# Fewer feed-forward items per step in the first half of a softmax-statistics loop, more in the second

## The chip, the cores and the metric

The kernel runs on all 8 cores of one Trainium2 chip, each core on its own two sequences of the batch of 16. The metric is device time in microseconds of the slowest core.

## The reference

One layer adds to its input x (16 x 2048 x 1024, float32) an attention block and a feed-forward block, both on the same layer norm of x:

```python
xn = _layernorm(x, axis=-1)
x = x + attn(xn, W_kqv, W_o) + ffn(xn, W_r, W_k, W_v, mu_r, mu_k)
# attn: 16 heads of 64, rotary embedding on Q and K, causal softmax(QK^T/8) V, then @ W_o.T
# ffn:  xr = mu_r*xn + (1-mu_r)*xn_prev ; xk = mu_k*xn + (1-mu_k)*xn_prev
#       r  = sigmoid(xr @ W_r.T) ; k = square(relu(xk @ W_k.T)) ; out = r * (k @ W_v.T)
```

## The kernel before

Each core works through 8 tiles of 512 tokens, four to a sequence: `for seq in range(2): for J in range(4)`. J says how much causal history the tile has: its keys fill J+1 chunks of 512. A tile is worked in this order:

1. the output projection of the tile before (`wo_emit`, L759), then the K, Q and V projections (L377 and L434);
2. the **statistics loop** (L552 to L622), 16 heads x 4 query blocks of 128 = 64 steps, s = 4h + qtl. A step computes the scores of one query block against all its keys: on TensorE one matmul of 64 rows for each chunk of 512 keys (L567; for J = 3 L591 and L610), the last chunk cut to 128 (qtl+1) columns; on VectorE the causal mask is added to its diagonal block (L573, L597); on ScalarE an exponential over the row, whose accumulated sum is all that is kept (L578; L602 and L616). Score banks are reused after one to three steps, depending on J;
3. the softmax sums become an extra row of Q, and the attention loop proper runs (L699 scores, L709 exponential, L686 product with V).

The feed-forward work of the tile is a list of 246 small closures, `ffn_work`, each of which issues about one instruction. After every step of the statistics loop `drain_ffn(k)` takes the next k of them off the list, so that they stand behind that step's matmuls on TensorE's queue, behind its mask add on VectorE's and behind its exponential on ScalarE's. The engines work their queues strictly in the order written; the only waits are on semaphores. The list in order:

- one subtraction over the whole tile (L455) and 8 multiply-adds of 512 columns (L459), on VectorE: they make the input `xrk` of the r projection from `call`;
- the r projection: 64 matmuls of 128 rows and 512 columns (L476), after each 8 of them an epilogue: Tanh on ScalarE (L486) and a scaling on VectorE (L489);
- 8 multiply-adds on VectorE (L512). They overwrite `xrk` with the input of the k projection, so they wait for the last matmul of the r projection, and the first matmul of the k projection waits for the last of them;
- the k projection: 64 matmuls and 8 epilogues of two VectorE instructions (L495, L499) which write `call`; the v projection needs all of them;
- the v projection: 64 matmuls and 8 epilogues of one VectorE instruction (L505); a last addition (L519).

The matmuls of the projections alternate between PSUM banks 6 and 7, by groups of 8. Twelve weight loads (one for 16 matmuls, SyncE's queue, in the first tile GpSimd's with a store behind it) stand in the list 30 items ahead of their first use, into five buffers. Whatever is left of the list after step 63 is issued by `drain_ffn(n_ffn)`.

With the numbers of before, 3 items per step for s < 32 and 7 after that, the list falls on the steps so:

| steps | items |
|---|---|
| 0 to 3 | two loads, L455, the 8 of L459, 1 matmul |
| 4 to 28 | the other 63 matmuls of the r projection, its epilogues, 4 loads |
| 29 to 31 | the 8 of L512, 1 matmul of the k projection |
| 32 to 53 | the other 127 matmuls, their epilogues, 6 loads, L519 |
| 54 to 63 | none |

Of the kernel before, what the change touches and what calls it, by code (L numbers as in the profile page):

```python
# [133 lines left out]
def build_program():  # L134
# [223 lines left out]
    for seq in range(BSEQ):  # L358
        for J in range(NJ):
# [186 lines left out]
            def drain_ffn(k):  # L546
                while ffn_i[0] < n_ffn and k > 0:
                    ffn_work[ffn_i[0]]()
                    ffn_i[0] += 1
                    k -= 1  # L550

            for h in range(H):  # L552
                for qtl in range(4):
                    s = 4 * h + qtl
# [29 lines left out]
                    else:  # L584
# [24 lines left out]
                        for chn in (0, 1):  # L609
# [9 lines left out]
                            accum_out=sgm[:, 4 * h + qtl: 4 * h + qtl + 1]),  # L619
                          reads=bksL + ["consts"],  # L620
                          writes=["attn0", "attn1", "sgm"])
                    drain_ffn(3 if s < 32 else 7)  # L622
            drain_ffn(n_ffn)
            if ln_phases:
                ln_phases[0]()
# [231 lines left out]
if __name__ == "__main__":  # L857
    nc = build_program()
    print("built ok, instructions:", sum(1 for _ in nc.all_instructions()))
```

How the kernel before makes its waits and increments, by code:

```python
            def run(eng):  # L118
                for s in by_eng[ename]:
                    for sm, v in s.waits:
                        eng.wait_ge(handles[sm], v)
                    inst = s.fn(eng)
                    if s.inc_on:
                        inst.then_inc(handles[s.sem], s.inc)
```

## Time and profile before

| | |
|---|---|
| time, median of 2 runs | 3136.86 us (3132.43 to 3141.3) |
| the profiled execution | 3133.19 us |
| its span on the slowest core (core 2) | 3131.6 us |
| spans of the 8 cores | 3100.7 to 3131.6 us |
| PE busy | 2264.8 us (72%) |
| ACT busy | 1351.3 us (43%) |
| DVE busy | 1246.2 us (40%) |
| granted clock, mean over the span | 0.752 (core 2) |

PE is TensorE, ACT is ScalarE, DVE is VectorE, POOL is GpSimd and SP is SyncE. A granted clock of 1.00 is 2.4 GHz and 0.50 is 1.2 GHz; a value between them is a mean over a stretch that has both. The clock in force decides how long a matmul takes, so a busy share of PE means little without it. A step of the statistics loop starts where the first weight load of its score matmul (L567 or L591) starts; all stretches below are cut at such starts.

### The profile page before, as it was taken

To read this page: it belongs to the slowest core of one execution; us is meant where nothing else is said; L and a number is where in the kernel's file an instruction comes from. 1 tells how busy PE (TensorE), PEld (TensorE's weight loads), DVE (VectorE), ACT (ScalarE), POOL (GpSimd) and SP (SyncE) were. 2 spreads that over 40 slices of the span, in tenths; PEclk is the share of its full clock that TensorE was granted. 3 is DMA by queue.
4 is the path that set the end of the run, shared out by engine and by line. 5 is a ranking of instruction groups with operands and counts; after the bars stand their busy time and mean duration, and the time that the engine had idled before them with its cause. 6 is when DMAs were issued, how large, how long until landed. Compare 5 with 4: busy or idle time off the path is not lost.

```text
span 3131.6 us, 33119 instructions; the slowest of 8 cores (3100.7 to 3131.6 us)
## 1 busy us (share of the span) xinstructions
PE 2264.8 (72%) x8148; PEld 780.8 (25%) x8232; DVE 1246.2 (40%) x2429; ACT 1351.3 (43%) x2729; POOL 101.9 (3%) x125
## 2 busy tenths in 40 slices
PE   1466577677886886977886656767868778798787
PEld 0122131222322222222232212222322222312232
DVE  5444554444432344222344455444443233613122
ACT  0033305551365632776631330444316655077674
POOL 0210010000000001000000000000010000100000
PEclk8787586867677787578788857876776778858687
DMA  4696052103311024100024203310141100500000
GB/s 74 88 168 122 1 151 62 50 0 101 88 34 41 1 75 101 34 24 31 1 81 108 67 9 105 93 56 10 67 108 44 46 1 14 148 26 23 28 1 27
DMA packets 83743, 180.67 MB, mean 58 GB/s; under 512 B 5592, under 2 KB 50792, under 8 KB 81512
## 3 DMA queue, kind: packets, MB, share of 16 engines
q1 hardware_dynamic: 34448, 121.78, 11.5%
q0 software_dynamic: 49120, 56.77, 11.3%
q8 instruction: 84, 1.38, 0.2%
q14 instruction: 91, 0.75, 0.1%
HBM read 153.23 MB, written 31.59 MB: 59 GB/s over the span
## 4 chain that ended last, share of the span: by engine, by line
PE 54%; DVE 19%; issue 9%; DMA 8%; ACT 8%; POOL 1%; DVEq 0%; ACTq 0%; POOLq 0%; SPq 0%
PE ps L476 13%; PE ps L686 11%; PE ps L699 9%; PE ps L567 6%; PE ps L759 4%; DMA qtil<-call 3%; PE ps L610 3%; DVE call L395 3%; ACT attn L578 3%; PE ps L591 2%; DMA ktil<-call 2%; DVE srowt L736 2%; ACT p L709 2%; PE ps L377 2%; DVE attn L731 1%
## 5 line engine op out<-in xcount | busy, mean ns | idle before, releaser
L709 ACT ACTIVATE p<-ps 128x512 bf16<-128x512 f32 (+3 forms) x1280 | 589.7, 533 | 471.1 <-PE ps L699 469.4
L578 ACT ACTIVATE attn<-ps 128x128 bf16<-128x128 f32 (+11 forms) x384 | 331.9, 864 | 880.8 <-DVE ps L573 589.0
L686 PE MATMUL ps<-p,vtok 128*65 128x512 bf16 (+3 forms) x1280 | 487.6, 419 | 102.4 <-DVE p L716 46.8
L699 PE MATMUL ps<-qtil,ktil 65*128 65x512 bf16 (+3 forms) x1280 | 425.8, 431 | 48.6 <-DMA qtil<-augh 48.6
L476 PE MATMUL ps<-xrk,wbuf 128*128 128x512 bf16 x984 | 338.5, 466 | 50.2 <-DVE xrk L512 40.9
L377 PE MATMUL ps<-xn,wbuf 128*128 128x512 bf16 x1008 | 254.5, 398 | 147.3 <-DVE qtil L403 100.9
L567 PE MATMUL ps<-ktil,qtil 64*128 64x512 bf16 (+3 forms) x768 | 254.3, 426 | 128.1 <-ACT attn L578 59.1
L716 DVE TENSOR_TENSOR p<-p,tri 128x128 bf16<-128x128 bf16 x512 | 109.3, 225 | 577.2 <-ACT p L709 570.6
L686 PEld LDWEIGHTS ps<-p,vtok 128*65 128x65 bf16 x1280 | 162.9, 128 | 410.5 <-issue 380.1
L602 ACT ACTIVATE attn<-ps 128x640 bf16<-128x640 f32 (+3 forms) x128 | 110.6, 864 | 233.4 <-PE ps L610 201.1
L573 DVE TENSOR_TENSOR ps<-ps,maskadd 128x128 f32<-128x128 f32 x384 | 107.6, 295 | 254.0 <-PE ps L567 252.9
L699 PEld LDWEIGHTS ps<-qtil,ktil 65*128 65x128 bf16 x1280 | 138.5, 113 | 227.3 <-issue 178.0
L377 PEld LDWEIGHTS ps<-xn,wbuf 128*128 128x128 bf16 x1024 | 97.4, 102 | 304.4 <-issue 215.8
L476 PEld LDWEIGHTS ps<-xrk,wbuf 128*128 128x128 bf16 x1024 | 85.1, 106 | 303.4 <-issue 261.4
L395 DVE TENSOR_TENSOR call<-ps,rsigt 128x512 bf16<-128x512 f32 x128 | 88.5, 691 | 140.7 <-DMA ktil<-call 89.8
L434 PE MATMUL ps<-wbuf,xn 128*128 128x256 bf16 x1024 | 118.4, 275 | 32.1 <-DMA wbuf<-wkqvt 22.4
L616 ACT ACTIVATE attn<-ps 128x1024 bf16<-128x1024 f32 x128 | 131.1, 1024 | 19.1 <-PE ps L591 0.4
L476 PE MATMUL ps<-call,wbuf 128*128 128x512 bf16 x500 | 128.9, 389 | 13.9 <-DVE call L499 12.4
L759 PE MATMUL ps<-attn,wbuf 128*128 128x512 bf16 x496 | 131.5, 424 | 4.8 <-DVE attn L670 3.2
L567 PEld LDWEIGHTS ps<-ktil,qtil 64*128 64x128 bf16 x768 | 59.3, 102 | 301.1 <-issue 292.9
L610 PE MATMUL ps<-ktil,qtil 64*128 64x512 bf16 x256 | 113.9, 539 | 24.2 <-ACT attn L602 14.7
L670 DVE TENSOR_TENSOR attn<-attn,ps 128x512 bf16<-128x512 bf16 x64 | 44.0, 687 | 211.0 <-PE ps L666 209.1
(96 smaller groups left out, 1819.1 us busy)
## 6 DMA issues: line engine op xcount, KB each, us to landing
wbuf<-wtmp SPq DMA_DIRECT2D x196, 512.0 KB, 3.8
y<-outb POOLq DMA_DIRECT2D x8, 2048.0 KB, 7.5
wtmp<-wbuf SPq DMA_DIRECT2D x28, 512.0 KB, 6.8
ktil<-call POOLq DMA_DIRECT2D x32, 256.0 KB, 9.0
qtil<-call POOLq DMA_DIRECT2D x32, 256.0 KB, 9.6
outb<-x POOLq DMA_DIRECT2D x7, 1024.0 KB, 19.8
wbuf<-wkqvt POOLq DMA_DIRECT2D x12, 512.0 KB, 19.8
rsigt<-ropemaps SPq DMA_DIRECT2D x8, 512.0 KB, 4.1
```

Source lines behind the costliest of these rows:

```text
L377: A("T", lambda e, slot=slot, fc2=fc2, ci=ci, bk=bk: e.matmul(bank(bk), wb3[slot][:, ci, 128 * fc2:128 * fc2 + 128], xn3[:, ci, 1:513], st ...
L395: A("V", lambda e, gch=gch, bk=bk: e.tensor_tensor(out=call3[:, gch, :], in0=bank(bk), in1=mapblk[:, 512:1024], op=OP.mult), reads=[bkey, ...
L434: A("T", lambda e, slot=slot, tt=tt, ci=ci, bk=bk: e.matmul(ps[:, 512 * bk: 512 * bk + 256], xn3[:, ci, 1 + 128 * tt:1 + 128 * tt + 128], ...
L476: "T", lambda e, holder=holder, fc2=fc2, ci=ci, bk=bk, rhs3=rhs3: e.matmul(bank(bk), wb3[holder["slot"]][:, ci, 128 * fc2:128 * fc2 + 128] ...
L567: A("T", lambda e, h=h, qtl=qtl, chn=chn, N=N, base=base: e.matmul(ps[:, 512 * (base + chn): 512 * (base + chn) + N], qt_ap[0:64, 512 * h ...
L578: A("S", lambda e, kext=kext, h=h, qtl=qtl, base=base: e.activation(attn[:][:, 0:kext], ps[:, 512 * base: 512 * base + kext], AF.Exp, scal ...
L610: A("T", lambda e, h=h, qtl=qtl, chn=chn, pL=pL: e.matmul(ps[:, 512 * (pL + chn): 512 * (pL + chn) + 512], qt_ap[0:64, 512 * h + 128 * qtl ...
L616: A("S", lambda e, h=h, qtl=qtl, pL=pL: e.activation(attn[:][:, 0:1024], ps[:, 512 * pL: 512 * pL + 1024], AF.Exp, scale=1.0 / 32.0, accum ...
L686: A("T", lambda e, h=h, kti=kti, qs=qs, pb=pb, j=j, nkt=nkt: e.matmul(ps[0:65, 512 * (2 + j) + qs: 512 * (2 + j) + 512], vt_ap[:, 65 * H * ...
L699: A("T", lambda e, h=h, kti=kti, qs=qs, sbk=sbk: e.matmul(ps[:, 512 * sbk + qs: 512 * sbk + 512], kt_ap[0:65, T * h + 128 * kti: T * h + 1 ...
L709: A("S", lambda e, kti=kti, qs=qs, sbk=sbk, pb=pb: e.activation(p2[pb][:, qs:512], ps[:, 512 * sbk + qs: 512 * sbk + 512], AF.Exp, scale=0 ...
L759: A("T", lambda e, slot=slot, fc2=fc2, dc=dc, bk=bk: e.matmul(bank(bk), wb3[slot][:, dc, 128 * fc2:128 * fc2 + 128], attn3[:, dc, :], star ...
```

## The change

The two numbers of the drain after each step are altered, and nothing else: 2 items for s < 32 instead of 3, 8 items from s = 32 on instead of 7.

```diff
@@ -619,7 +619,7 @@
                             accum_out=sgm[:, 4 * h + qtl: 4 * h + qtl + 1]),
                           reads=bksL + ["consts"],
                           writes=["attn0", "attn1", "sgm"])
-                    drain_ffn(3 if s < 32 else 7)
+                    drain_ffn(2 if s < 32 else 8)
             drain_ffn(n_ffn)
```

By the count of the list, the items now fall on the steps so:

| steps | items |
|---|---|
| 0 to 5 | two loads, L455, the 8 of L459, 1 matmul |
| 6 to 31 | 44 matmuls of the r projection, 5 epilogues, 3 loads |
| 32 to 34 | 19 matmuls of the r projection, its last 3 epilogues, 1 load, 1 of L512 |
| 35 | 7 of L512, 1 matmul of the k projection |
| 36 to 54 | the other 127 matmuls, their epilogues, 6 loads, L519 |
| 55 to 63 | none |

## Rows read from the trace of the kernel before

**Rows 1.** The profile's page: clock in 40 slices; the chain by engine; weight loads.

```profile
PEclk8787586867677787578788857876776778858687
PE 54%; DVE 19%; issue 9%; DMA 8%; ACT 8%; POOL 1%; DVEq 0%; ACTq 0%; POOLq 0%; SPq 0%
wbuf<-wtmp SPq DMA_DIRECT2D x196, 512.0 KB, 3.8
```

**Rows 2.** Busy time by stretch: steps 0 to 5; J=0 and J=3.

```profile
core 2: us, PE busy (x) PEld busy (x) DVE busy (x) ACT busy (x) POOL busy (x), PEclk, DMA share, GB/s
176.61:190.12 13.51, 3.77 (x17) 1.25 (x15) 10.06 (x17) 2.48 (x10) 1.75 (x2) 0.61 1.17 214
...
1223.65:1239.96 16.31, 12.07 (x29) 2.75 (x30) 9.44 (x15) 10.94 (x22) 0.00 (x0) 0.51 0.27 77
```

**Rows 3.** Busy time by stretch: steps 6 to 28; J=0 to 3, all eight.

```profile
190.12:215.40 25.28, 22.00 (x81) 6.15 (x81) 8.26 (x27) 15.74 (x50) 2.62 (x3) 0.94 0.93 173
483.53:522.73 39.20, 35.06 (x104) 7.21 (x104) 10.41 (x31) 26.62 (x53) 0.00 (x0) 0.72 0.12 41
831.54:886.38 54.84, 51.65 (x127) 10.85 (x127) 10.98 (x31) 36.56 (x54) 0.00 (x0) 0.56 0.09 29
1239.96:1307.99 68.03, 65.05 (x149) 13.65 (x150) 11.08 (x30) 52.13 (x101) 0.00 (x0) 0.50 0.07 24
...
sum 371.03, PE 339.86 PEld 75.08 DVE 81.10 ACT 261.27 POOL 2.62; mean PE 42.48 PEld 9.39 DVE 10.14 ACT 32.66 POOL 0.33
```

**Rows 4.** Busy time by stretch: steps 29 to 31; J=0 and all eight.

```profile
215.40:226.81 11.41, 1.49 (x7) 0.40 (x6) 8.31 (x16) 3.96 (x14) 0.87 (x1) 0.72 0.88 184
...
sum 83.06, PE 29.16 PEld 5.65 DVE 58.79 ACT 45.61 POOL 0.87; mean PE 3.64 PEld 0.71 DVE 7.35 ACT 5.70 POOL 0.11
```

**Rows 5.** Busy time by stretch: steps 32 to 53; J=0, J=3, all eight.

```profile
226.81:264.95 38.14, 36.23 (x146) 12.84 (x149) 19.20 (x44) 10.94 (x42) 3.18 (x4) 0.95 0.65 111
...
1318.02:1373.18 55.16, 51.90 (x211) 16.73 (x215) 19.46 (x45) 43.77 (x85) 0.00 (x0) 0.95 0.09 30
...
sum 375.28, PE 357.15 PEld 117.89 DVE 155.05 ACT 206.84 POOL 3.18; mean PE 44.64 PEld 14.74 DVE 19.38 ACT 25.85 POOL 0.40
```

**Rows 6.** Busy time by stretch: steps 54 to 63 and the sums' end, all eight.

```profile
sum 161.66, PE 84.99 PEld 15.95 DVE 56.30 ACT 116.97 POOL 0.00; mean PE 10.62 PEld 1.99 DVE 7.04 ACT 14.62 POOL 0.00
```

**Rows 7.** Timeline (start, duration), PE, J=3: six matmuls before and after the clock rises.

```profile
1320.03 2.74 PE L476 MATMUL ps<-xrk,wbuf 128*128 128x512 bf16 x6
...
1323.71 1.47 PE L476 MATMUL ps<-xrk,wbuf 128*128 128x512 bf16 x6
```

**Rows 8.** Timeline, all engines, J=0: between the r and the k projection.

```profile
218.41 0.59 ACT L486 ACTIVATE ps<-ps 128x512 f32<-128x512 f32 x1
219.11 0.69 DVE L489 TENSOR_SCALAR rsigt<-ps 128x512 bf16<-128x512 f32 x1 [2.22 <-ACT ps L486]
219.71 0.29 DVE L573 TENSOR_TENSOR ps<-ps,maskadd 128x128 f32<-128x128 f32 x1
219.91 2.45 DVE L512 SCALAR_TENSOR_TENSOR xrk<-call,mu2s,xn 128x512 bf16<-128x512 bf16 x3
...
226.79 0.59 PE L476 MATMUL ps<-xrk,wbuf 128*128 128x512 bf16 x1 [8.17 <-DVE xrk L512]
```

**Rows 9.** Timeline, ACT, steps without items: exponentials four steps apart, J=0, 2, 3.

```profile
270.65 0.28 ACT L578 ACTIVATE attn<-ps 128x128 bf16<-128x128 f32 x1
273.36 0.28 ACT L578 ACTIVATE attn<-ps 128x128 bf16<-128x128 f32 x1
...
952.91 1.13 ACT L578 ACTIVATE attn<-ps 128x1152 bf16<-128x1152 f32 x1 [0.23 <-DVE ps L573]
960.12 1.13 ACT L578 ACTIVATE attn<-ps 128x1152 bf16<-128x1152 f32 x1 [0.20 <-ACT attn L578]
...
1382.30 0.70 ACT L602 ACTIVATE attn<-ps 128x640 bf16<-128x640 f32 x1 [0.20 <-PE ps L610]
...
1391.98 0.70 ACT L602 ACTIVATE attn<-ps 128x640 bf16<-128x640 f32 x1 [0.20 <-PE ps L610]
```

## The prediction

> **What bounds the kernel now.** I began with the page. TensorE ends most of the chain (54%), and its granted clock in the 40 slices swings between 0.5 and 0.9 [rows 1]. The list is in every case the same 246 items, so a time can only change through three things: the clock at which the moved matmuls run, what ScalarE and VectorE can do beside them, and the waits at the seams. So I cut the statistics loop of all eight tiles at the step starts and read busy time and clock of each stretch.
>
> Steps 6 to 28 (2 to 3 items of matmul each): PE is busy 65.05 of 68.03 us at J = 3, all of it at the lower level of the clock, 1.2 GHz; at J = 2 the mean grant is 0.56, at J = 1 0.72 and at J = 0 0.94 [rows 3]. Steps 29 to 31 belong to VectorE: 8.31 us busy of 11.41 at J = 0, with PE busy 1.49 [rows 4]. Steps 32 to 53 (7 items) run at 0.95, nearly all at 2.4 GHz, with PE busy 36.23 of 38.14 us at J = 0 and 51.90 of 55.16 at J = 3 [rows 5]. After the list has run dry the step is ScalarE's: at J = 3 four steps take 1391.98 - 1382.30 = 9.68 us, 2.42 each; at J = 2 1.80; at J = 0 0.68 [rows 9]. For J = 1 I interpolate 1.2.
>
> The price of one feed-forward matmul at either level: six take 2.74 us at the low one and 1.47 at the high one [rows 7]. A single one at the low level takes 0.59 [rows 8], so the spacing there is (2.74 - 0.59)/5 = 0.43 us and 0.16 of each burst is its end running out; at the high level the spacing is (1.47 - 0.16)/6 = 0.22 us.
>
> **The change part by part.** Counts of items are those of the two tables ahead.
>
> *Steps 0 to 5 hold 5 matmuls fewer.* VectorE's work before the first matmul is unchanged but for two more mask adds of 0.29 us [rows 8]; the other steps' scores pass beside it. At J = 0 before, 2.95 us lay between the first matmul (with the DVE chain about 10.6 us long, from 10.06 us busy) and step 6 at 13.51 [rows 2]; six matmuls at 0.43 were in it, now one: -2.5 and +0.6, so -2.0. At J = 1 and 2 the scores of two more steps also pass under VectorE: -3.2 and -3.8. At J = 3 ScalarE's 2.42 a step takes over, five of them and a start of about 1: 13.0 for 16.31, so -3.3. Two sequences: 2 x 12.3 = **-24.6**.
>
> *Steps 6 to 31: three steps more, 14 matmuls fewer (44 for 58), 3 epilogues fewer.* At J = 3 what is not a feed-forward matmul costs (68.03 - 58 x 0.43)/23 = 1.88 a step. After: 68.0 + 3 x 1.88 - 14 x 0.43 = 67.6; some 0.6 less for the missing epilogues, 67.0. ScalarE would need 26 x 2.42 and five times Tanh's 0.59 = 65.9, so it binds almost equally, and the removed matmuls buy nothing more. J = 2: 54.84 + 3 x 1.31 - 6.0 = 52.8; a bit over half of its steps could lose the clock's better moments, so 53.7. J = 1: 39.20 now (37.3 in the other sequence). All at 1.2 GHz the same reckoning, 44 x 0.43 plus 26 x 0.91, gives 42.6; all at 2.4 ScalarE's floor of 26 x 1.2 and some epilogues gives 33. J = 0: 31.5 and 23.5 in the same way, against 25.28 now. In each J fewer columns pass per step, and the rows say that the stretch with a smaller part of feed-forward matmuls among its PE work is granted less (0.94, 0.72, 0.56, 0.50 for J = 0 to 3, at the same three items) [rows 3]. So I let each J fall towards the next one: J = 1 40, J = 0 27. Sum 2 x (27 + 40 + 53.7 + 67) = 375.4 against 371.0: **+4.4**.
>
> A rule that speaks against this part is in the Trainium skill, page "TensorE: Matmul & The Clock Gate", section "A second HAM failure mode: psum-queue depth-cycling": small idle times of PE between groups of matmuls make the clock swing between its levels, and the cost is paid in the bursts after. The grant of 0.72 at J = 1 agrees with it. By the rule alone J = 0 and J = 1 would be at the low level throughout, and this part would be +18 instead of +4.
>
> *Steps 29 to 31 become step 35.* From the Tanh of the last epilogue to the first k matmul 226.79 - 218.41 = 8.4 us pass at J = 0: Tanh, scaling, eight multiply-adds and three mask adds [rows 8]. The chain is what it was but for two mask adds: 7.8, with the matmuls at both ends 8.4. What changed is that three steps' scores and exponentials passed beneath it, and now one does; that is in the step counts. At J = 2 and 3 the Tanh stands behind its step's own exponentials, so I take 8.9 and 9.5 there. 2 x 35.2 = 70.4 for 83.1: **-12.7**. All else queued on VectorE waits: mask 35, so ScalarE idles some 5 us and PE 7.
>
> *The dense stretch.* Steps 32 to 34 and 36 to 54 are 22 steps as before, with 19 matmuls more. At 2.4 GHz they cost 19 x 0.216 = 4.1 a tile, +32.8. That stretch now starts with r matmuls, straight from the low clock (J = 1 to 3), and after step 35's idle PE climbs a second time. Before, the clock rose 4.7 us after the idle at J = 3 (between the two rows of [rows 7]; work began at about 1318.0). 4 to 4.5 us at half speed lose 2.2: six tiles, and 1 at J = 0: +15.2. At J = 3 ScalarE has slack no more under PE's longer steps, which gives 1.5 back twice: -3. Sum **+45.0** on 375.3 [rows 5].
>
> *The last steps:* one fewer in each tile at ScalarE's floor, 0.68 + 1.2 + 1.80 + 2.42, twice: **-12.1** (of 161.7 [rows 6]).
>
> *At nothing:* the weight loads. They keep their lead of 30 items. Eight items take at least 1.9 us, so the lead is 7 us against a landing of 3.8 [rows 1]. Without that cover a load would cost PE the difference at 12 places a tile. In the first tile GpSimd loads from float32 instead; PE's whole idle time in the dense stretch there is 38.14 - 36.23 = 1.9 us [rows 5], so no load is late by more than that now, and its lead stays. Nothing moves past a DMA issue that another part waits for.
>
> **Sum:** -24.6 + 4.4 - 12.7 + 45.0 - 12.1 = 0.0 on a span of 3131.6 and an execution of 3133.2. The median of the runs stands 3.7 above that execution, so 3137.
>
> **Rivals.**
> *A, the slower side: the clock.* Steps 6 to 31 stay at 1.2 GHz at J = 0 and 1 (2 x (4.5 + 2.6 + 1) = +16), and both climbs of the dense stretch take twice as long (+13). For it: J = 3 and mostly J = 2 do so today; against: at J = 0 0.94 is far from it. With something for ScalarE waiting behind step 35, 3160. It decides as soon as J = 0 is granted under 0.6 in steps 6 to 31.
> *B, faster: the matmuls saved are saved.* J = 0 and 1 keep their grants (2 x (3.5 + 6) = -19), and the first climb takes no loss at some tiles: 3115. For it: 0.94 at J = 0 leaves the low level only a moment there. Against: a smaller share of matmuls.
> *C, much slower: the dense stretch stays low after step 35.* 113 matmuls x 0.21 in eight tiles = +190, 3325. Against it: after an equal idle of 8.17 us [rows 8] the stretch is granted 0.95.
> *D, the change does nothing at the seams:* the 8 multiply-adds hidden as before would leave out the loss of step 35; excluded by their order, since only one step is left beside them.
>
> **How the numbers follow.** My forecast, gains and losses within 12 us of each other, 0.5; A 0.24; B 0.22; C 0.02; D and the rest 0.02. The predicted time is 3137. The unknown terms are the grants (-19 to +16), the second climb (-13 to +13) and step 35 (8 x 1 either way); they don't all fall on one side, and the runs of before differ by 9. Range 3112 to 3163, which takes in A and B. A measurement of this kernel can tell about 2%, 63 us, from no change; that is 8 us a tile, and only C reaches it on the slow side, nothing on the fast side. Faster 0.01, same 0.96, slower 0.03.
>
> **What would show it.** Right: steps 6 to 31 at J = 3 take 66 to 68 us; step 35 8.4 to 9.5; the idle of L476 put down to L512 grows from 8.17 at J = 0 only little there but to 6 or 7 at J = 3; steps 32 to 54 without 35 take 5 to 8 us more at every J, with two climbs of the clock at J = 1 to 3; J = 2 and 3 win a little in all, J = 1 loses. Wrong: a grant over 0.85 at J = 1 in steps 6 to 31 (B), under 0.6 at J = 0 (A), or step 35 under 7 us, which would mean that its chain is not serial.

## The result, and the profile after

| | before | after |
|---|---|---|
| time, median of all runs | 3136.49 us (11 runs) | 3164.70 us (12 runs) |
| ratio, 95% interval | | 1.009 (1.0068 to 1.0113) |
| the same kernel timed again beside another set of before | 3134.15 us (34 runs) | 3173.27 us (11 runs), 1.0107 (1.0073 to 1.0142) |

By the ratios the change makes the kernel 28 to 34 us slower. That is within the 2% of which the prediction gave "same" 0.96, but it is a clear loss where 3137 was forecast, and 1.7 us outside the range. Some executions are disturbed and longer, among them the first profile of the changed one (3210.59 us, with the granted clock at 0.81 for 575 to 765 us of each core, a value that the trace of before never shows), and the ratios leave them out. All rows of after below are from the second profile, `after_again`; where rows are of core 2, so are those of before. The marks of all stretches, before and after, stand 0.50 us ahead of the first weight load of their step; the lengths are those of the steps.

The page of `after_again`, slowest core (core 1): span, PE's busy time, clock, chain by engine, and the matmuls of the projections (L476) with what PE waited for. The last line is the same group before, core 2.

```profile
span 3171.7 us, 33173 instructions; the slowest of 8 cores (3138.6 to 3171.7 us)
PE 2336.8 (74%) x8232; PEld 789.5 (25%) x8232; DVE 1250.9 (39%) x2429; ACT 1350.5 (43%) x2729; POOL 101.9 (3%) x125
PEclk8777585867667687588787757686775877858687
PE 57%; DVE 18%; issue 8%; ACT 8%; DMA 7%; POOL 1%; DVEq 0%; ACTq 0%; POOLq 0%; SPq 0%
L476 PE MATMUL ps<-xrk,wbuf 128*128 128x512 bf16 x1024 | 381.8, 494 | 92.7 <-DVE xrk L512 65.2
...
L476 PE MATMUL ps<-xrk,wbuf 128*128 128x512 bf16 x984 | 338.5, 466 | 50.2 <-DVE xrk L512 40.9
```

ACT's and DVE's busy times are those of before. PE has the same instructions (the trace of before has 984 of the 1024 matmuls of L476) and takes longer for them, 494 ns for 466 by the mean of this group. The stretches show where. First steps 6 to 31 of the changed kernel on core 2 (the columns are those of [rows 2]): J = 0 to 3, the second J = 0, and all eight.

```profile
181.23:213.04 31.81, 30.83 (x69) 5.88 (x71) 10.07 (x30) 17.07 (x56) 1.75 (x2) 0.50 0.75 160
480.61:523.72 43.11, 41.97 (x95) 6.57 (x97) 10.19 (x30) 27.93 (x58) 0.00 (x0) 0.50 0.07 25
830.02:887.15 57.13, 53.03 (x120) 10.42 (x123) 10.38 (x30) 39.02 (x58) 0.00 (x0) 0.50 0.06 19
1238.10:1310.45 72.35, 64.83 (x147) 12.34 (x149) 10.67 (x31) 57.81 (x111) 0.00 (x0) 0.50 0.05 15
1707.90:1734.52 26.62, 25.50 (x68) 5.51 (x70) 8.46 (x27) 15.73 (x52) 0.00 (x0) 0.63 0.13 40
...
sum 404.43, PE 376.21 PEld 69.75 DVE 81.00 ACT 282.55 POOL 1.75; mean PE 47.03 PEld 8.72 DVE 10.13 ACT 35.32 POOL 0.22
```

Against [rows 3]: J = 1 has lost its high clock altogether (0.72 to 0.50), J = 0 most of it (0.94 to 0.50 and 0.63). By the mean of the eight cores the grants were 0.94, 0.80, 0.58 and 0.50 and are 0.60 and three times 0.50. At J = 0 six of the sixteen tiles stay at 0.50 throughout and take 31.8 us, the others rise for a part of the stretch. J = 3 had no high clock to lose, and still takes 72.35 us.

The sums over the eight tiles of the other stretches, in order: steps 0 to 5, 32 to 34, 35, 36 to 54, 55 to the end of the loop.

```profile
sum 93.62, PE 41.62 PEld 10.02 DVE 75.87 ACT 51.68 POOL 1.75; mean PE 5.20 PEld 1.25 DVE 9.48 ACT 6.46 POOL 0.22
sum 68.77, PE 66.16 PEld 20.24 DVE 18.86 ACT 39.10 POOL 0.87; mean PE 8.27 PEld 2.53 DVE 2.36 ACT 4.89 POOL 0.11
sum 76.74, PE 9.99 PEld 2.22 DVE 55.08 ACT 24.76 POOL 0.87; mean PE 1.25 PEld 0.28 DVE 6.89 ACT 3.09 POOL 0.11
sum 359.89, PE 343.38 PEld 117.06 DVE 150.67 ACT 176.69 POOL 3.18; mean PE 42.92 PEld 14.63 DVE 18.83 ACT 22.09 POOL 0.40
sum 149.13, PE 74.72 PEld 14.04 DVE 51.56 ACT 106.02 POOL 0.00; mean PE 9.34 PEld 1.76 DVE 6.44 ACT 13.25 POOL 0.00
```

Set against the terms of the prediction, in us. Beside core 2 stand means of the cores' own sums, of all eight and of cores 4 to 7 alone: in this execution cores 0 to 3 were granted 0.81 for 104 to 151 us each, cores 4 to 7 never.

| term | forecast | core 2 | mean of 8 cores | mean of cores 4 to 7 |
|---|---|---|---|---|
| steps 0 to 5 | -24.6 | -26.1 | -25.5 | -25.8 |
| steps 6 to 31 for 6 to 28 | +4.4 | +33.4 | +32.7 | +32.0 |
| step 35 for 29 to 31 | -12.7 | -6.3 | -5.6 | -4.6 |
| the dense stretch | +45.0 | +53.4 | +47.8 | +43.2 |
| the last steps | -12.1 | -12.5 | -12.6 | -12.6 |
| sum | 0.0 | +41.8 | +36.8 | +32.2 |

Two terms failed, the second by 28 us and the third by 7 to 8. A mean over the cores by J shows that the failure is spread evenly: the whole statistics loop takes 105.3, 128.2, 155.7 and 184.8 us at J = 0 to 3, where it took 100.5, 123.6, 150.9 and 180.6. That is 4.2 to 4.8 us in every tile (3.4 to 4.5 on cores 4 to 7), whatever its clock was before, which suggests more than one cause.

Below, a tile's stretch without rows is such a mean of the eight cores from their traces.

### The profile page after: what moved, and what is told of

The parts are those of the page before. It is cut to its first block, busy times and chain, and to the rows that moved or that the text cites. A ratio compares the mean times of both kernels' runs of the same rounds, so it can differ in the third digit from the quotient of the medians.

```text
span 3209.1 us, 33173 instructions; the slowest of 8 cores (3180.6 to 3209.1 us)
## 1 busy us (share of the span) xinstructions
PE 2396.2 (75%) x8232; PEld 806.4 (25%) x8232; DVE 1251.5 (39%) x2429; ACT 1354.2 (42%) x2729; POOL 101.8 (3%) x125
## 4 chain that ended last, share of the span: by engine, by line
PE 60%; DVE 17%; issue 8%; ACT 7%; DMA 6%; POOL 1%; DVEq 0%; ACTq 0%; POOLq 0%; SPq 0%
PE ps L476 15%; PE ps L686 11%; PE ps L699 9%; PE ps L567 7%; PE ps L759 4%; PE ps L377 3%; PE ps L610 3%; DMA ktil<-call 2%; PE ps L591 2%; PE ps L434 2%; DVE call L395 2%; DVE srowt L736 2%; ACT p L709 2%; DMA qtil<-call 2%; ACT attn L578 2%
## 5 line engine op out<-in xcount | busy, mean ns | idle before, releaser
L476 PE MATMUL ps<-xrk,wbuf 128*128 128x512 bf16 x1024 | 391.0, 505 | 91.0 <-DVE xrk L512 64.8
L377 PE MATMUL ps<-xn,wbuf 128*128 128x512 bf16 x1024 | 279.1, 429 | 133.9 <-DVE qtil L403 96.7
L567 PE MATMUL ps<-ktil,qtil 64*128 64x512 bf16 (+3 forms) x768 | 279.4, 462 | 60.8 <-ACT attn L578 44.2
L602 ACT ACTIVATE attn<-ps 128x640 bf16<-128x640 f32 (+3 forms) x128 | 110.7, 865 | 252.3 <-DVE ps L597 125.4
L476 PEld LDWEIGHTS ps<-xrk,wbuf 128*128 128x128 bf16 x1024 | 89.8, 109 | 339.7 <-issue 315.5
L434 PE MATMUL ps<-wbuf,xn 128*128 128x256 bf16 x1024 | 131.3, 295 | 28.3 <-DMA wbuf<-wkqvt 19.4
L476 PE MATMUL ps<-call,wbuf 128*128 128x512 bf16 x512 | 139.3, 415 | 12.4 <-DVE call L499 12.4
L759 PE MATMUL ps<-attn,wbuf 128*128 128x512 bf16 x512 | 139.2, 436 | 3.2 <-DVE attn L670 3.2
```

Of the source, the lines that this page charges most:

```text
L377: A("T", lambda e, slot=slot, fc2=fc2, ci=ci, bk=bk: e.matmul(bank(bk), wb3[slot][:, ci, 128 * fc2:128 * fc2 + 128], xn3[:, ci, 1:513], st ...
L434: A("T", lambda e, slot=slot, tt=tt, ci=ci, bk=bk: e.matmul(ps[:, 512 * bk: 512 * bk + 256], xn3[:, ci, 1 + 128 * tt:1 + 128 * tt + 128], ...
L476: "T", lambda e, holder=holder, fc2=fc2, ci=ci, bk=bk, rhs3=rhs3: e.matmul(bank(bk), wb3[holder["slot"]][:, ci, 128 * fc2:128 * fc2 + 128] ...
L567: A("T", lambda e, h=h, qtl=qtl, chn=chn, N=N, base=base: e.matmul(ps[:, 512 * (base + chn): 512 * (base + chn) + N], qt_ap[0:64, 512 * h ...
L759: A("T", lambda e, slot=slot, fc2=fc2, dc=dc, bk=bk: e.matmul(bank(bk), wb3[slot][:, dc, 128 * fc2:128 * fc2 + 128], attn3[:, dc, :], star ...
```

## The experiments

**Which of the two numbers, and which tiles.** Each kernel is the one of before with this one line changed.

```diff
-                    drain_ffn(3 if s < 32 else 7)
+                    drain_ffn(2 if s < 32 else 7)                    # first_only
+                    drain_ffn(3 if s < 32 else 8)                    # second_only
+                    drain_ffn((2 if s < 32 else 8) if J < 2 else (3 if s < 32 else 7))   # low_J
+                    drain_ffn((2 if s < 32 else 8) if J >= 2 else (3 if s < 32 else 7))  # high_J
```

`after_again`: 

> The changed kernel once more, for a profile beside those of the next runs. Timed it was 1.009 of before. Its first profile holds the tiles J = 0 and 1 at a granted 0.50 to 0.6 in steps 6 to 31 (before: 0.94 and 0.72). Theory 'clock': here again, 28 to 29 us at J = 0 and 43 at J = 1 for that stretch (before 25 and 38 to 39). Rival 'dense part': that stretch is as long as before in sum (371 us) and the loss stands in steps 32 to 54.

Measured 1.0107; steps 6 to 31 28.9 us at J = 0, 43.1 at J = 1. At J = 0 and 1 it is as the clock theory had it; that J = 2 and 3 lose as much is not in it.

`first_only`: 

> 2 items for s < 32 and 7 after. Theory 'clock': the first number carries the whole loss, since it alone decides the clock of steps 6 to 31; ratio to before 1.007 to 1.011. Rival 'dense part': eight items per step are what costs, then this stands at 1.000 to 1.003.

Measured 1.0098 (1.0067 to 1.0130), as much as the whole loss within the intervals: the first number alone makes it.

`second_only`: 

> 3 items for s < 32 and 8 after. Theory 'clock': nothing of the loss, 0.999 to 1.003; the list is dry three steps earlier, which at J = 3 costs about 2 us a tile since those steps are then ScalarE's alone. Rival 'dense part': 1.006 or more.

Measured 1.0032 (0.9999 to 1.0064), between the two and nearer to nothing. The loops took 1 to 3 us more a tile at every J, not only at J = 3; no run says why.

`low_J`: 

> The change at J = 0 and J = 1 alone, 3 and 7 at J = 2 and 3. Theory 'clock': most of the loss is here, because only these tiles had a high clock to lose: 1.006 to 1.009. Rival 'seam and ScalarE' (r projection cut by the dense part, a second climb of the clock, Tanh behind ScalarE's exponentials, all larger at J = 2 and 3): 1.001 to 1.004 here and the rest at J = 2 and 3.

Measured 1.0047 (1.0016 to 1.0079): the value is below what the clock theory wanted, and the interval reaches over it. By the value, half of the loss is elsewhere.

`high_J`: 

> The change at J = 2 and J = 3 alone. The traces so far put 4.2 to 4.9 us of loss on each of the eight tiles, whatever J. Theory now, 'two causes of equal size': at J = 0 and 1 the low clock of steps 6 to 31, at J = 2 and 3 ScalarE, whose Tanh makes a round trip over VectorE that PE had hidden with its third item. Then this is 1.004 to 1.006, as much as the change at J = 0 and 1 alone (1.0047). Rival 'clock alone': 1.000 to 1.002, since J = 2 and 3 ran at 0.5 before as well.

Measured 1.0031 (1.0004 to 1.0059). The value is below the expected one and the interval reaches over it; "clock alone", which wanted no loss here, stays possible by the time alone. The trace says more: the loops take 154.3 and 184.9 us at J = 2 and 3, for 150.9 and 180.6. J = 2 had a mean grant of 0.58 before and has 0.50 here, so the clock can have a part in its loss; at J = 3 the grant is 0.50 in both, and the 4.3 us there have another cause. With `low_J` it adds up to 1.0078, for 1.009 and 1.0107 of the whole.

**What J = 3 loses without a clock to lose.** In `after_again`, core 2, J = 3, a Tanh's neighbourhood (timeline: start, duration; weight loads left out):

```profile
1252.84 1.28 ACT L486 ACT_TABLE_LOAD   x1
...
1253.82 0.71 PE L591 MATMUL ps<-ktil,qtil 64*128 64x512 bf16 x2
1254.13 0.58 ACT L486 ACTIVATE ps<-ps 128x512 f32<-128x512 f32 x1
1254.82 0.69 DVE L489 TENSOR_SCALAR rsigt<-ps 128x512 bf16<-128x512 f32 x1 [4.78 <-ACT ps L486]
1255.43 0.49 DVE L597 TENSOR_TENSOR ps<-ps,maskadd 128x128 f32<-128x128 f32 x2
1255.81 1.02 ACT L602 ACTIVATE attn<-ps 128x1024 bf16<-128x1024 f32 x1 [1.09 <-DVE ps L597]
...
1257.28 1.01 PE L610 MATMUL ps<-ktil,qtil 64*128 64x512 bf16 x2 [2.75 <-ACT attn L602]
```

The scaling (L489) waits for the Tanh; the mask add of the next step stands behind the scaling on VectorE's queue; ScalarE, done with the Tanh, stands idle for 1.09 us until that mask add has come; and PE waits 2.75 us for a bank that the exponential frees. A Tanh thus costs a round trip from ScalarE over VectorE and back. (In this first one of the tile, the load of a function table, 1.28 us, stands ahead of it and is a part of PE's wait.) The same wait of ScalarE's comes once for every Tanh of the stretch. These are the lines on who waited around L602 at J = 3, core 2, first of before in steps 6 to 28 with its seven Tanhs, then of `after_again` in steps 6 to 31 with five (us in all, times):

```profile
  DVE ps L597: 7.7, 7
who waited for it (us, times):
  PE ps L610: 1.6, 1
...
  DVE ps L597: 5.5, 5
who waited for it (us, times):
  PE ps L610: 5.5, 4
```

ScalarE waits 1.1 us a Tanh in both. PE waited behind one of seven before and waits behind four of five now: that is what the third item had hidden.

Two pairs test the round trip. The first leaves the Tanh out in both kernels:

```diff
             def sig_epi(fco, bk, bkey):
-                A("S", lambda e, bk=bk: e.activation(
-                    bank(bk), bank(bk), AF.Tanh, scale=0.5),
-                  reads=[bkey, "consts"], writes=[bkey])
```

`after_no_tanh`: 

> The changed kernel without the Tanh on ScalarE; it leaves the sigmoid out, so r is a linear function of its projection. Theory 'ScalarE round trip': at J = 3 steps 6 to 31 fall from 72.6 us to 65 or 66 (44 x 0.43 + 26 x 1.77 = 64.9, PE alone), at J = 2 from 57.2 to 54; at J = 0 and 1, where PE at 1.2 GHz binds anyway, 28 to 30 and 43 as now. Rival 'PE and ScalarE bind equally': less than 3 us less at J = 3, since ScalarE's exponentials alone need 26 x 2.42 = 62.9 and collide with PE as before.

`before_no_tanh`: 

> The kernel before without the Tanh, the pair of after_no_tanh; it leaves the same part out. Theory 'ScalarE round trip': with a third item PE hid most of it, so steps 6 to 28 at J = 3 fall only from 68.0 to 65.5 or 66, and the changed kernel's loss in that stretch at J = 3 (4.6 us) goes to zero within 1 us. Rival: it falls by as much as the changed one does, and the loss stays above 3 us.

Core 2, steps 6 to 31 of `after_no_tanh` at J = 1 and 3, where the columns are those of [rows 2]:

```profile
480.37:523.27 42.90, 41.92 (x95) 6.55 (x97) 10.69 (x30) 23.91 (x50) 0.00 (x0) 0.50 0.08 25
...
1228.57:1293.88 65.31, 63.99 (x147) 13.17 (x149) 11.00 (x31) 54.10 (x105) 0.00 (x0) 0.50 0.05 17
```

Steps 6 to 28 of `before_no_tanh` at the same J and core:

```profile
469.18:497.62 28.44, 28.14 (x103) 6.55 (x104) 10.96 (x30) 20.85 (x44) 0.00 (x0) 0.88 0.18 56
...
1188.55:1254.13 65.58, 64.58 (x149) 14.38 (x150) 11.43 (x30) 47.61 (x94) 0.00 (x0) 0.50 0.07 25
```

At J = 3 both come to PE's own time, 65.3 and 65.6, and the loss of 4.6 us is gone (-0.3), as the round trip wanted. At J = 1 the changed kernel gains nothing, PE at 1.2 GHz binds it; the one of before falls from 39.20 to 28.44 us, and its grant rises to 0.88. Without Tanh the profiled executions take 3122.75 us for the changed kernel and 3071.13 us for the one of before (two more of the latter were of the longer kind, 3143.70 and 3149.47; there is no interval): the loss at J = 3 in this stretch is gone, and the loss at J = 1 is larger. Leaving the Tanh out takes its 0.59 us and the table load away too, so this pair alone does not single out the round trip; the last pair does.

**The clock, with work added.** The changed kernel and one thrown-away matmul per step at J = 0:

```diff
                     drain_ffn(2 if s < 32 else 8)
+                    if J == 0 and 5 <= s < 32:
+                        A("T", lambda e: e.matmul(bank(5), i128[:], xn3[:, 0, 1:513],
+                                                  start=True, stop=True),
+                          reads=["i128", "xn"], writes=["ps5"])
```

`pad_J0`: 

> The changed kernel with one more matmul (128 rows, 512 columns, thrown away) in each of the steps 5 to 31 at J = 0: work is added, nothing is left out. Theory 'clock': with as many matmul columns per step as before, J = 0 is granted 0.85 or more in steps 6 to 31 (0.58 to 0.64 without), and that stretch takes 26 to 29 us, no longer than the 28 to 29.6 without the 26 added matmuls. Rival 'the clock has nothing to do with it': the grant stays near 0.6 and the stretch grows by 26 x 0.43 = 11 us to 40.

Core 2, steps 6 to 31, the two tiles with J = 0:

```profile
186.78:214.61 27.83, 26.27 (x95) 7.27 (x96) 8.09 (x27) 16.02 (x52) 1.75 (x2) 0.91 0.86 171
...
1707.81:1734.40 26.59, 25.32 (x95) 7.19 (x96) 8.09 (x27) 16.02 (x52) 0.00 (x0) 0.94 0.12 40
```

26 matmuls more (x95 for x69) and four microseconds less than the 31.81 of the first tile, at a grant of 0.91 for 0.50. Over the eight cores the pair is 27.8 and 27.5 us for 29.6 and 28.2. None of the sixteen tiles stays at 0.50, where six did. So one more matmul a step is enough to bring the high clock at J = 0. It makes up for itself there, and no more than that. No such run was made at J = 1.

**Order, denser first.** `flat7` drains 7 after every step. `dense_first` drains 7 too, but 3 while VectorE's multiply-adds are at the head of the list, so that each block of them is shared by three steps:

```diff
+            def drain_dense(few, many):
+                left = few if id(ffn_work[min(ffn_i[0], n_ffn - 1)]) in spread else many
+                dense = left == many
+                while ffn_i[0] < n_ffn and left > 0:
+                    if dense and id(ffn_work[ffn_i[0]]) in spread:
+                        break
+                    drain_ffn(1)
+                    left -= 1
...
-                    drain_ffn(3 if s < 32 else 7)
+                    drain_dense(3, 7)
```

(`spread` holds L455 and the multiply-adds of L459 and L512.)

`flat7`: 

> 7 items after every step until the list is dry (step 35). Theory 'a sparse part is paid at the low clock': the r projection now runs as densely as the k and v projections and is granted 0.9 or more once it has started, at every J; the 29 steps left are ScalarE's at 0.7, 1.2, 1.8 and 2.4 us. By those prices J = 0 stays at 100, J = 1 and 2 gain 3 to 5 us each, and J = 3 gains nothing, since both blocks of VectorE multiply-adds fall on one or two steps and ScalarE starves beneath them: ratio 0.993 to 0.998. Rival 'the order of the items does not matter, only their number does': 1.000.

`dense_first`: 

> 7 items per step, but 3 while VectorE's multiply-adds are at the head of the list, so that three steps share each block of them; the list is dry at about step 39. Theory: as flat7, and at J = 2 and 3 the exponentials of three steps pass beneath each block: J = 0 100, J = 1 121, J = 2 147, J = 3 174 us for the statistics loop (before: 100.5, 123.6, 150.9, 180.6), ratio 0.989 to 0.994. Rival 'ScalarE's round trip costs the same in a dense r projection': J = 3 stays over 178 and the ratio at 0.996 or more.

Measured 1.0126 (1.0094 to 1.0157) and 0.9982 (0.9961 to 1.0004), both worse than expected. The clock came: on core 2, `flat7`, steps 4 to 11, in the dense r projection, J = 0 and J = 3:

```profile
193.42:207.76 14.34, 13.38 (x57) 4.55 (x56) 5.88 (x14) 7.39 (x23) 2.62 (x3) 1.00 1.08 174
...
1245.47:1272.69 27.22, 20.78 (x81) 6.01 (x80) 5.65 (x14) 19.49 (x38) 0.00 (x0) 0.94 0.18 58
```

At J = 3 eight steps take 27.22 us, 3.4 each, where ScalarE's exponentials need 2.42: in a dense r projection three steps in four have a Tanh, and ScalarE waits for a mask add 6 times in these eight, 1.1 us each. The rival named for `dense_first` was right (J = 3 at 180.8 us, over 178), while J = 1 and 2 came to 122.2 and 148.3, near the expected 121 and 147. The rest of `flat7`'s loss is its two blocks of multiply-adds, about 11 us on a single step each, with scores and exponentials held up behind them: spreading these over three steps is worth 1.0126 against 0.9982.

**The round trip taken out.** The scaling is issued five items after its Tanh; nothing is left out.

```diff
+            late = []
...
-                return A("V", lambda e, fco=fco, bk=bk: e.tensor_scalar(
+                late.append([6, lambda: A("V", lambda e, fco=fco, bk=bk: e.tensor_scalar(
                     out=rsig3[:, fco, :], in0=bank(bk),
                     scalar1=0.5, scalar2=0.5, op0=OP.mult, op1=OP.add),
-                  reads=[bkey], writes=["rsigt"])
+                  reads=[bkey], writes=["rsigt"])])
...
                     ffn_i[0] += 1
                     k -= 1
+                    for it in late:
+                        it[0] -= 1
+                    while late and late[0][0] <= 0:
+                        late.pop(0)[1]()
```

`late_37` (drains 3 and 7): 

> The kernel before (3 and 7) with one thing moved: the scaling on VectorE that follows a Tanh is issued five items later, so that the mask adds of the next one or two steps no longer stand behind it; Tanh and everything else stay. Theory 'round trip': what a Tanh costs is the mask add that waits behind its scaling, not its own 0.59 us. Then the statistics loops lose most of the 70 us that leaving Tanh out took away (less 8 x 1.3 for the table load that remains and the Tanhs themselves): J = 3, steps 6 to 28, 68.0 to 66 or 67; J = 0 and 1 25.3 and 38 to 23 and 31; ratio 0.980 to 0.988. Rival 'ScalarE is simply full': what counts is Tanh's time on ScalarE, nothing changes, 0.997 to 1.000.

`late_28` (drains 2 and 8): 

> The changed kernel (2 and 8) with the same scaling five items later. Theory 'two causes': the part of the loss at J = 3 and 2 that is the round trip goes (steps 6 to 31: 72.6 to 66 to 68, 57.2 to 54 to 55), the part at J = 0 and 1 that is the low clock stays (29 and 43), and the wait for the multiply-adds shortens by the Tanh and scaling ahead of them (step 35: 9 to 10.7 down to 8 to 8.5): 1.000 to 1.004 of the kernel before, and at least 40 us behind late_37. Rival 'the clock follows the round trips': J = 0 and 1 get the high level back here too, 29 to 24 and 43 to 35.

`late_37` is 0.9906 (0.9889 to 0.9923): faster than both kernels, though not by the 0.980 to 0.988 expected. `late_28` is 0.9999 (0.9986 to 1.0013), some 29 us behind it, where at least 40 were expected. The same place as above, the first Tanh at J = 3, in `late_28`, core 2 (its lines stand further down: L487 is the Tanh, L490 the scaling, L602 the mask add, L607 and L615 the exponential and the score matmul):

```profile
1245.89 1.28 ACT L487 ACT_TABLE_LOAD   x1
...
1247.18 0.58 ACT L487 ACTIVATE ps<-ps 128x512 f32<-128x512 f32 x1
1247.68 1.02 ACT L607 ACTIVATE attn<-ps 128x1024 bf16<-128x1024 f32 x1
1247.90 0.30 DVE L602 TENSOR_TENSOR ps<-ps,maskadd 128x128 f32<-128x128 f32 x1 [2.17 <-PE ps L596]
1248.11 0.68 DVE L490 TENSOR_SCALAR rsigt<-ps 128x512 bf16<-128x512 f32 x1
```

The exponential follows the Tanh at once, its mask add long done. Steps 6 to 31 of `late_28`, core 2, at J = 1 and 3:

```profile
478.37:521.27 42.90, 42.90 (x97) 6.55 (x97) 9.93 (x29) 27.72 (x58) 0.00 (x0) 0.50 0.08 25
...
1231.44:1298.24 66.80, 65.42 (x150) 13.09 (x149) 10.56 (x31) 57.46 (x111) 0.00 (x0) 0.50 0.05 16
```

Steps 6 to 28 of `late_37`, core 2, at J = 1 to 3:

```profile
477.49:510.22 32.73, 32.48 (x106) 6.95 (x104) 10.71 (x31) 25.07 (x52) 0.00 (x0) 0.78 0.15 49
813.93:855.72 41.79, 37.36 (x129) 9.31 (x127) 11.16 (x31) 36.00 (x54) 0.00 (x0) 0.85 0.12 38
1210.01:1276.11 66.10, 65.74 (x152) 14.25 (x150) 11.33 (x30) 52.23 (x102) 0.00 (x0) 0.50 0.08 24
```

In `late_28` J = 3 falls from 72.35 to 66.80 us with Tanh and its table load still there, and ScalarE's waits of 1.1 us for a mask add are gone, all five. J = 1 stays at 42.90 us and 0.50, though PE has no gap left there at all: the two causes apart in one kernel. J = 0 is 27.5 us by the mean of the eight cores (28.9 in `after_again`), with six of sixteen tiles at 0.50 throughout in both; the rival's 24 did not come. J = 2 is 54.8 us for 57.2. Step 35 falls to 8.0 to 8.3 us at every J.

In `late_37` PE has hardly a gap left at J = 1 and 3, and J = 1 and 2 fall from 39.20 and 54.84 to 32.73 and 41.79 us, at J = 2 with a grant of 0.85 for 0.56. So with the round trip out the change costs as much as before (0.9906 to 0.9999), but elsewhere: by the mean of eight cores the loops of `late_28` are 5.7, 11.4 and 7.2 us longer than those of `late_37` at J = 0 to 2, and 2.1 us shorter at J = 3.

What `late_37` missed: its loops lost 45 us by the mean of eight cores, where the expectation wanted most of 70 less 10. Leaving the Tanh out had also taken away a second table load in each tile, ahead of the logarithm that ends the loop (L634), and so 8 x 1.28 us more than counted. And in this execution cores 0 to 3 were granted 0.81 for 263 to 308 us each, 54 to 97 of them in the dense stretch, which took 391 us there for 376 of before; on cores 4 to 7, never at 0.81, it took 377 for 376, and the loops lost 50.

## Why the prediction was wrong

- **What bounds the kernel, prices of a matmul, steps 0 to 5, the dense stretch, the last steps:** right, within 1 to 3 us on sums of 12 to 45. The second climb of the clock is there: step 36, behind the idle of step 35, is at 0.50 in all eight tiles of core 2 (3.32 us at J = 0, 4.60 at J = 3).
- **Steps 6 to 31, J = 0 and 1:** the step that failed is "so I let each J fall towards the next one", which gave 27 and 40. Measured 28.9 and 43.1 (+10 in all): J = 1 fell to the bottom, and at J = 0 six of sixteen tiles did. `pad_J0` shows the clock as the cause at J = 0, and at J = 1 the rows of `late_28` do, with PE busy for all of 42.90 us at 0.50. Rival A had the mechanism of this half, and about its size, with a chance of 0.24; its own terms add up to 3137 + 16 + 13 = 3166, while the prediction wrote 3160 and ended its range at 3163. The Trainium skill's rule ("TensorE: Matmul & The Clock Gate", "A second HAM failure mode: psum-queue depth-cycling") speaks of a clock that swings between its levels where PE idles shortly between groups of matmuls; that J = 0 and 1 would be low throughout, +18, was the prediction's own reading of it. This case agrees in part: with some of the short waits of PE taken out, `late_37` is granted more at J = 2 (0.85 for 0.56 on core 2). It does not account for J = 1 of `late_28`, which neither swings nor has a gap.
- **Steps 6 to 31, J = 2 and 3:** forecast 53.7 and 67.0, measured 57.2 and 72.6, +18 over four tiles. The step that failed is "ScalarE would need 26 x 2.42 and five times Tanh's 0.59 = 65.9, so it binds almost equally". It added up ScalarE's instructions and left out the table load of 1.28 us and ScalarE's wait at each Tanh, five of 1.1 at J = 3: 65.9 + 1.3 + 5.5 = 72.7, for the 72.6 measured. PE, with three items a step, had been slow enough to cover most of that; with two it is not. Removing PE work uncovered a chain through two other engines. No rival had it. At J = 2 the round trip is 2.4 of the 3.5 us missed (57.2 to 54.8 in `late_28`); the rest was not taken apart.
- **Step 35:** forecast 8.4, 8.4, 8.9, 9.5; measured 9.0, 9.3, 9.8 and 10.7. The likely cause is the same round trip: the last Tanh stands behind an exponential whose mask add stands behind the scaling of the Tanh before. With the scaling late the step is 8.0 to 8.3 us, but that moves the last scaling out from ahead of the multiply-adds as well, so the two are not told apart.
- **The range** took in the grants, the climbs and step 35, but gave the ScalarE term no bound at all. That term (+18) and the clock of J = 0 and 1 (+10) alone lead from 3137 to 3165, just out of it. What J = 1 would have saved with two items at its old grant was not measured: no run holds that.
- **The signs named:** of those for "right", J = 3 at 66 to 68 us failed (72.6), and so did a gain at J = 2 and 3 (both lost 4 to 5 us a tile). The sign of rival A, J = 0 under 0.6 in steps 6 to 31, stood on its edge: 0.60 by the mean of the eight cores.

## What to carry to other kernels

Filler instructions that cross engines (matmul, Tanh on one engine, scaling on another) cost more than their durations: whatever is queued behind the last link waits for the whole chain, so issue that link a step or two later. When work is taken off the engine that binds, add up the waits of the next one as well as its instructions. And before thinning out matmuls, look at the clock that the stretch is granted: here the thinner stretch ran them at half the speed at J = 1 and for most of J = 0.

## What the runs showed of the hardware

- At J = 0, 26 more matmuls of 128 x 512 in 26 steps raised the grant from 0.50 and 0.63 to 0.91 and 0.94 (core 2, `pad_J0`) and made the stretch shorter or as long.
- A busy PE can stay at the low level: at J = 1 of `late_28`, core 2, PE is busy for 42.90 of 42.90 us with matmuls of 64 and 128 rows, all at 0.50.
- A third value of the granted clock, 0.81, is in some profiles, and not always on all cores: in `late_37` it was in force for 263 to 308 us on each of cores 0 to 3, in `after_again` 104 to 151, and in both nothing on cores 4 to 7; none in the one of before. In `after_again`, core 2, step 49 with its 8 matmuls took 2.04 us at 1.00 in the first J = 0 tile and 2.44 at 0.81 in the second.
- ScalarE loads a table twice in each tile, 1.28 us each: before the first Tanh (L486), and before the logarithm behind the last exponential (L634). There is none between a Tanh and the exponentials after it, and without Tanh both are gone (17 loads on core 2 in `after_again`, 1 in `after_no_tanh`). At J = 3 the step of the first Tanh takes 2.47 us without Tanh, 3.97 with load and Tanh but a late scaling (`late_28`), and 5.37 with the round trip too (`after_again`).
